# Scratch tables with each partition's rows in one run, and four store buffers for the isolated blocks' h rows

## What is computed

```python
x = _layernorm(x + _L0(x))   # MLP 64-128-64 on every node, then a GCN sum over edges
x = _layernorm(x + _L1(x))   # GCN, relu, GCN, weighted by edge_weight
x = _layernorm(x + _L2(x))   # GAT: softmax over each node's incoming edges
x = _layernorm(x + _L3(x))   # message MLP per edge (src, dst, edge_attr), sum, update MLP

# e.g. the sum over edges in L0; the others differ in the weight of a message
msgs = h[src] * norm[:, None]
out = jax.ops.segment_sum(msgs, dst, num_segments=n) + b2
```

## Time and profile before

| | us |
|---|---|
| median of 3 runs (2938.37 to 2942.83) | 2941.12 |
| the profiled execution | 2938.16 |
| its span, first to last instruction | 2936.4 |
| POOL busy in it | 2169.0 (74%) |
| PE busy | 2171.1 (74%) |
| DVE busy | 1984.6 (68%) |
| ACT busy | 1429.8 (49%) |

### The profile page before, as it was taken

The page is one execution under the profiler, slowest core; times in us unless marked ns, Lnnn a source line. Parts: engine busy times, 40 slices in busy tenths (PEclk is TensorE's granted clock), DMA queues, the critical chain, the costliest instruction groups (busy, mean ns, idle before and its releaser), DMA issues.

```text
span 2936.4 us, 39046 instructions
## 1 busy us (share of the span) xinstructions
PE 2171.1 (74%) x10332; PEld 1155.7 (39%) x10332; DVE 1984.6 (68%) x3848; ACT 1429.8 (49%) x2755; POOL 2169.0 (74%) x1666
## 2 busy tenths in 40 slices
PE   3998899968778757777687759998356576666665
PEld 1444444434445324444343434444155233333332
DVE  6665688858888747777599968998699343333332
ACT  2877677745444436665344437777222232223332
POOL 7888878778888268886788858888233688888887
PEclk9999999979898768888789979999555787777777
DMA  7998522224556455555344445555477322222221
GB/s 210 285 271 241 144 57 54 59 58 93 129 130 141 93 128 125 128 133 125 78 112 113 111 95 127 141 137 125 94 191 186 77 62 52 55 57 57 54 53 26
DMA packets 624033, 338.13 MB, mean 115 GB/s; under 512 B 536606, under 2 KB 585100, under 8 KB 623817
## 3 DMA queue, kind: packets, MB, share of 16 engines
q1 hardware_dynamic: 550217, 288.96, 39.1%
q0 software_dynamic: 73600, 46.68, 9.4%
HBM read 203.61 MB, written 130.80 MB: 114 GB/s over the span
## 4 chain that ended last, share of the span: by engine, by line
POOL 57%; issue 19%; PE 9%; DVE 8%; DMA 3%; SPq 1%; ACT 1%; DVEq 0%; POOLq 0%; ACTq 0%
POOL g_row L857 42%; POOL x_with_info L864 8%; POOL out_rows L864 8%; PE bank L1075 2%; PE bank L1098 1%; DVE rT L1685 1%; PE bank L984 1%; PE pair L1055 1%; DMA g_row<-t_x,gidx 1%; PE pair L984 1%; DMA g_row<-in_x,dst_i 1%; DVE x_r L1662 1%; DVE ss L1608 1%; PE pair L1066 0%; DVE w_r L2007 0%
## 5 line engine op out<-in xcount | busy, mean ns | idle before, releaser
L857 POOL DMA_INDIRECT g_row<-t_x,gidx x600 | 808.1, 1347 | 258.6 <-issue 217.3
L1281 ACT ACTIVATE hid<-pair,b_up 128x1000 f32<-128x1000 f32 x375 | 406.0, 1083 | 42.9 <-PE pair L1056 42.1
L1076 PE MATMUL bank<-hid,w_dn 128*64 128x500 f32 x750 | 420.8, 644 | 0.0
L1075 PE MATMUL bank<-hid,w_dn 128*64 128x500 f32 x750 | 420.7, 644 | 0.0
L1055 PE MATMUL pair<-xT,w_top 64*128 64x500 f32 x550 | 316.7, 657 | 15.5 <-ACT hid L1281 15.0
L857 POOL DMA_INDIRECT g_row<-x_with_info,src_i x200 | 275.3, 1377 | 63.8 <-issue 55.8
L1056 PE MATMUL pair<-xT,w_bot 64*128 64x500 f32 x550 | 317.5, 658 | 0.0
L857 POOL DMA_INDIRECT g_row<-t_h,gidx x200 | 261.5, 1307 | 75.7 <-issue 75.7
L857 POOL DMA_INDIRECT g_row<-in_x,dst_i x200 | 261.1, 1306 | 68.7 <-issue 68.1
L1262 ACT ACTIVATE xT<-bank 128x500 f32<-128x500 f32 x275 | 160.2, 583 | 295.3 <-DVE rT L1685 163.2
L864 POOL DMA_INDIRECT out_rows<-n_r,fidx x200 | 248.8, 1244 | 61.6 <-issue 60.3
(11 more groups left out here) (257 smaller groups left out, 5205.0 us busy)
## 6 DMA issues: line engine op xcount, KB each, us to landing
x_in<-in_x_cols SPq DMA_DIRECT2D x100, 250.0 KB
x_with_info<-wide SPq DMA_DIRECT2D x50, 476.0 KB
wide<-in_x SPq DMA_DIRECT2D x50, 448.0 KB
out_rows<-x_r SPq DMA_DIRECT2D x100, 224.0 KB
l_k<-keep_row SPq DMA_DIRECT2D x150, 125.0 KB
l_a<-t_x SPq DMA_DIRECT2D x150, 112.0 KB
l_k<-on_row SPq DMA_DIRECT2D x50, 250.0 KB
t_x<-x_r SPq DMA_DIRECT2D x100, 112.0 KB
```

The costliest lines, as they stand in the source:

```text
L857: return g.indirect_dma_start(out=to, out_offset=None, in_=table, in_offset=bass.IndirectOffsetOnAxis(ap=index[:, tile:tile + 1], axis=0), ...
L1075: T.matmul(run.down[0:D, 0:CH], w_dn[a.stage][:, 0:D], hid[a.b2][:, 0, :], start=True, stop=True)
L1076: T.matmul(run.down[D:128, 0:CH], w_dn[a.stage][:, 0:D], hid[a.b2][:, 1, :], start=True, stop=True)\
L1281: A.activation(hid[a.b2][:, :, :], run.up[a.b2][:, :, 0:CH], ACT.Relu, bias=b_up[:, a.stage:a.stage + 1]).then_inc(Cn["hid"], 1)
```

## The change

1. `chunks` and `blocks` number the rows by partition: "(c p k) f" and "(b p j) f". The rows that one partition holds of a chunk (4, 1024 bytes) or block (8, 2048 bytes) are neighbours in the table. Level A's t1 rows, which a block holds as two chunks, go through a new view `chunk_pairs` (two pieces of 1024 bytes). `slot_id` and `gbase` are made with other patterns, so that gather indices follow. The loads of `half(l_a)` keep 256-byte pieces, since on the SBUF side the rows lie 512 bytes apart.
2. `in_pairs` is gone: an isolated block's store is two DMAs (`in_two`), not four.
3. `h2_r` has four buffers (the two `h0_r` are the first two), each with a semaphore of its own, `h2st0` to `h2st3`. The x2 stores count on three semaphores, one for each buffer `x2_r`. DVE's waits follow.

```diff
         def chunks(ap):
-            return ap.rearrange("(c k p) f -> c p k f", k=TC, p=R)
+            return ap.rearrange("(c p k) f -> c p k f", k=TC, p=R)
+
+        def chunk_pairs(ap):
+            return ap.rearrange("(b s p k) f -> b p s (k f)", s=2, k=TC, p=R)
 
         def blocks(ap):
-            return ap.rearrange("(b j p) f -> b p j f", j=TB, p=R)
+            return ap.rearrange("(b p j) f -> b p (j f)", j=TB, p=R)
...
-        h2_r = [b[0:R, :] for b in h2_r_all]
+        h2_r = [b[0:R, :] for b in h0_r_all + h2_r_all]
...
                     if a and a.stage == 0 and a.iso:
                         sp.wait_ge(Cn["rows"], normed(a))
-                        for to, frm in in_pairs(blocks(t1_d[E:2 * E, :])[a.b], x1_r[a.r4]):
+                        for to, frm in in_two(blocks(t1_d[E:2 * E, :])[a.b], x1_r[a.r4][:, :]):
                             sp.dma_start(to, frm).then_inc(s0_sem[a.b % 2], 16)
...
                         sp.wait_ge(Cn["h2b"], a.b + 1)
-                        for to, frm in in_pairs(blocks(t2_d[E:2 * E, :])[a.b], h2_r[a.b % 2]):
-                            sp.dma_start(to, frm).then_inc(s1_sem[a.b % 2], 16)
+                        for to, frm in in_two(blocks(t2_d[E:2 * E, :])[a.b], h2_r[a.b % 4][:, :]):
+                            sp.dma_start(to, frm).then_inc(h2_sem[a.b % 4], 16)
                         sp.wait_ge(Cn["rows"], normed(a))
-                        for to, frm in in_pairs(blocks(t3_d[E:2 * E, :])[a.b], x2_r[a.r3]):
-                            sp.dma_start(to, frm).then_inc(s1_sem[a.b % 2], 16)
+                        for to, frm in in_two(blocks(t3_d[E:2 * E, :])[a.b], x2_r[a.r3][:, :]):
+                            sp.dma_start(to, frm).then_inc(s1_sem[a.b % 3], 16)
...
-                for to, frm in in_two(blocks(t1_d[0:E, :])[b], n_view(a_rows[b % 2])):
+                for to, frm in in_two(chunk_pairs(t1_d[0:E, :])[b], a_rows[b % 2].rearrange("p (s c) -> p s c", s=2)):
...
-            g.iota(slot_id[:, :], pattern=[[R, NT]], base=1, channel_multiplier=1,
+            g.iota(slot_id[:, :], pattern=[[CH, NC], [1, TC]], base=1, channel_multiplier=TC,
-            g.iota(gbase[:, :], pattern=[[R, NT]], base=E, channel_multiplier=1,
+            g.iota(gbase[:, :], pattern=[[BLK, NI], [1, 2], [2, TC]], base=E, channel_multiplier=TB,
...
-                        at_least(dve, iso_sem1[a.b % 2], 128 * (a.b // 2))
-                        V.tensor_tensor(h2_r[a.b % 2][:, :], run.rows[a.b2][0:R, :], x1_r[a.r4][:, :], ALU.subtract).then_inc(Cn["h2"], 1)
+                        at_least(dve, Cn[f"h2st{a.b % 4}"], 32 * (a.b // 4))
+                        V.tensor_tensor(h2_r[a.b % 4][:, :], run.rows[a.b2][0:R, :], x1_r[a.r4][:, :], ALU.subtract).then_inc(Cn["h2"], 1)
...
                         if a.stage == 1 and a.s >= 3 and SEQ[a.s - 3].iso:
-                            par, times = iso_stored(a.s - 3)
-                            dve.wait_ge(iso_sem1[par], 128 * times)
+                            dve.wait_ge(iso_sem1[SEQ[a.s - 3].b % 3], 32 * (SEQ[a.s - 3].b // 3 + 1))
```

More of the change, by code:

```diff
@@ L446, in third_steps @@
                     yield step, (k - at) // 2
-        def in_pairs(dram_rows, buf):
-            to = dram_rows.rearrange("p (s k) f -> p s k f", s=2)
-            frm = buf.rearrange("p (k s f) -> p s k f", s=2, f=D)
-            return [(to[rows, s], frm[rows, s]) for rows in (slice(0, WIDE), slice(WIDE, R)) for s in range(2)]
         def in_two(to, frm):
@@ L601, in _ @@
             base_sem = [Cn["base0"], Cn["base1"]]
-            s0_sem, s1_sem = [Cn["s0st0"], Cn["s0st1"]], [Cn["s1st0"], Cn["s1st1"]]
+            s0_sem, s1_sem = [Cn["s0st0"], Cn["s0st1"]], [Cn[f"s1st{r}"] for r in range(3)]
+            h2_sem = [Cn[f"h2st{r}"] for r in range(4)]
             asked = [0]
@@ L632, in slot @@
                         sp.wait_ge(Cn["based"], a.b + 1)
-                        for to, frm in in_two(blocks(base0_d)[a.b], n_view(own_base[a.b % 2][:, :])):
+                        for to, frm in in_two(blocks(base0_d)[a.b], own_base[a.b % 2][:, :]):
                             sp.dma_start(to, frm).then_inc(base_sem[a.b % 2], 16)
@@ L664, in ld_a @@
                 at_least(sp, LA["t2"], b - 3)
-                for to, frm in in_two(n_view(a_base[b % 4]), blocks(base0_d)[b]):
+                for to, frm in in_two(a_base[b % 4], blocks(base0_d)[b]):
                     sp.dma_start(to, frm).then_inc(A_ld[b % 4].sem, 16)
@@ L739, in ld_third @@
             def ld_third(b):
-                for to, frm in in_two(n_view(third_in[b % 2]), blocks(t3_d[E:2 * E, :])[b]):
+                for to, frm in in_two(third_in[b % 2], blocks(t3_d[E:2 * E, :])[b]):
                     sp.dma_start(to, frm).then_inc(third_ld[b % 2], 16)
@@ L745, in third @@
                 if k < 0:
+                    for r in range(3):
+                        sp.wait_ge(s1_sem[r], 32 * len(range(r, NI, 3)))
                     for b in range(2):
-                        sp.wait_ge(s1_sem[b], 128 * len(range(b, NI, 2)))
                         ld_third(b)
@@ L751, in third @@
                         sp.wait_ge(F["rows"], b + 1)
-                        for to, frm in in_two(blocks(t4_d[E:2 * E, :])[b], n_view(third_out[b % 2])):
+                        for to, frm in in_two(blocks(t4_d[E:2 * E, :])[b], third_out[b % 2]):
                             sp.dma_start(to, frm).then_inc(third_st[b % 2], 16)
@@ L928, in _ @@
             for r in range(2):
[L930 removed]
+                pool.wait_ge([Cn["s0st0"], Cn["s0st1"]][r], 32 * len(range(r, NI, 2)))
             all_stored(pool, A_st, NI)
             gather_level(t1_d, B_ga, LB["msg"])
[L933 to L935 removed]
+            for r in range(4):
+                pool.wait_ge(Cn[f"h2st{r}"], 32 * len(range(r, NI, 4)))
             all_stored(pool, B_st)
@@ L1595, in _ @@
             assert c[1] == PREP_ALL
-            iso_sem0, iso_sem1 = [Cn["s0st0"], Cn["s0st1"]], [Cn["s1st0"], Cn["s1st1"]]
+            iso_sem0, iso_sem1 = [Cn["s0st0"], Cn["s0st1"]], [Cn[f"s1st{r}"] for r in range(3)]
             def chain(run):
@@ L1914, in _ @@
             for r in range(2):
-                dve.wait_ge(iso_sem0[r], 64 * len(range(r, NI, 2)))
-                dve.wait_ge(iso_sem1[r], 128 * len(range(r, NI, 2)))
+                dve.wait_ge(iso_sem0[r], 32 * len(range(r, NI, 2)))
+            for r in range(3):
+                dve.wait_ge(iso_sem1[r], 32 * len(range(r, NI, 3)))
+            for r in range(4):
+                dve.wait_ge(Cn[f"h2st{r}"], 32 * len(range(r, NI, 4)))
             for buf in l_ea:
```

11 lines of the change are left out of this document (4 added, 7 removed).

## The result

| | us |
|---|---|
| median after, 4 runs (2903.62 to 2918.97) | 2908.28 |
| median before, 4 runs (2938.37 to 2942.83) | 2940.21 |
| ratio, with its 95% interval | 0.9896 (0.9867 to 0.9925) |
| forecast | 2920.0 (2905 to 2934) |
| profiled execution after, and its span | 2918.97, 2917.2 |

The time lies inside the range, and the sign is right. The profiled execution, at 2918.97, gives nearly the forecast's number, but it is the slowest of the ten, and the ordinary time is 12 us lower. So two things have to be explained: whether the 19.2 us that this profile gained are the ones that the sum named, and where the others are.

A forecast was written before the change was run, and what follows sets the result against it. The prediction took POOL's own back-to-back gathers and scatters as the bound, leaving level starts and G to gain. Its terms, 15.8 + 1.9 + 3 = 20.7 us, took the median of 2941.12 to about 2920 (range 2905 to 2934).

The forecast's parts named there:

- the sum: Level A's end, h row wait gone: 15.8 us; shorter store landings: 1.9; level G: 3; together 20.7 us less.

The follow-up runs named there:

- the ten: All runs of the changed kernel: four with median 2908.28 us, and six of the same kernel without an edit, median 2905.19 us.
- The version with the PSUM scan: Changed kernel; in level M ACT writes its biased result to PSUM instead of SBUF, and DVE's first scan reads it there: 2894.56 us, ratio 0.9855.
- its two sets: Changed kernel, run twice without an edit between: four runs, 2908.28 us (0.9896), and six runs, 2905.19 us (0.9893).
- the mirror pair: Kernel before with only four h row buffers and own semaphores, 2922.07 us; the same with M's isolated rows gathered 2048 bytes apart, 2925.22 us.

## What to carry to other kernels

Where POOL issues indirect DMAs back to back and nothing seems to touch them, look at the long ones rather than at the mean, and at which DVE instruction ran as each began; a scan or an elementwise operation with both inputs in SBUF is the suspect, and giving one scan an input in PSUM took some 11 us off here. When a buffer's reuse waits on a queue that is itself held by another wait, more buffers are worth the stall, and a semaphore of its own was worth little of it (0.9 of some 6 us). And a delay on an engine with margin is not free as long as it shifts such instructions against each other.

The version with the PSUM scan beats both kernels: 2894.56 us (0.9855 of before), against 2905.19 and 2908.28 (0.9893 and 0.9896) for the changed kernel in its two sets, which were other groups.

## What the runs showed of the hardware

- A DVE scan of 64x500 values with two SBUF inputs (1.25 us) stretched each of POOL's indirect DMAs that began 0.10 to 0.65 us after its start, from 1.27 us to as much as 2.24 for a gather; the end came 1.08 to 1.10 us after the scan's for a gather, 1.00 to 1.05 for a put. Those that began in the 0.3 us ahead of the scan or in its first 0.09 us took 1.29 us at most, and the scan stayed at 1.25. With one input in PSUM none of the 7 that began in the same stretch took more than 1.27 (run with the PSUM scan).
- In level B of the kernel before, all 24 gathers above 1.6 us began during elementwise DVE instructions with two SBUF inputs (0.41 to 0.67 us long each); the longest took 2.46 us.
- SP took 0.81 us to issue a pair of loads with 256-byte pieces on both sides and 1.48 us for the same bytes with 1024-byte runs on the table's side and pieces on the SBUF side.
- Gathering isolated rows 256 bytes apart instead of 2048 left the changed kernel's M as it was (633.55 and 633.45 us); the mirror pair had 642.82 at 256 bytes and 637.72 at 2048, one profile each.
